# Side work of the first unit spread over later chunks, one table scatter per chunk, and matmuls of ones moved from the wait before the recurrent layer's output to the last down products

## The reference, cut to what matters

```
x = x + 0.5 * L0_ffn(layernorm(x))        # silu(x Wg) * (x Wu), hidden width 1024, then down to 256
x = x + L0_attn(layernorm(x))             # conv of 4 taps, two gates, linear recurrence over 512 steps, gelu gate
x = x + 0.5 * L0_ffn(layernorm(x))
x = x + 0.5 * L1_ffn(layernorm(x)) ...    # 8 experts; each adds 2048 deltas to a 256x256 matrix

# L0_attn: the decay is exp(-8 * sigmoid(gate) * softplus(a_param)), softplus on 256 numbers
# L1_ffn : deltas = softmax(expert_atom_weights) @ atoms     (8 x 2048)
#          weighted = deltas * sigmoid(importance)
#          added at (mask_idx // 256, mask_idx % 256); equal indices add up
```

## Time and profile before

| | us |
|---|---|
| three runs, median | 1249.54 |
| three runs, lowest and highest | 1244.13, 1250.32 |
| the profiled execution, its own time | 1241.68 |
| its span, first to last instruction | 1239.9 |
| TensorE busy | 1113.2 (90% of the span) |
| VectorE busy | 824.3 (66%) |
| GpSimd busy | 543.5 (44%) |
| mean granted TensorE clock | 0.973 |

### The profile page before, as it was taken

One profiled execution on the slowest core, in us unless ns is written; L12 is line 12 of the kernel. 1 busy time (PEld: TensorE's weight loads), 2 busy tenths in 40 slices (PEclk: granted clock), 3 DMA queues, 4 the chain that ended last, 5 costly groups with the idle time before them and its releaser, 6 DMA issues.

```text
span 1239.9 us, 22110 instructions
## 1 busy us (share of the span) xinstructions
PE 1113.2 (90%) x6837; PEld 939.2 (76%) x6837; DVE 824.3 (66%) x2280; ACT 603.3 (49%) x1420; POOL 543.5 (44%) x662
## 2 busy tenths in 40 slices
PE   3798779789989999998899989998899998999996
PEld 2677557677766778986676777896699997899995
DVE  3774456667888875567877876566766565665666
ACT  2234435351111334557766766555455554555552
POOL 4466445484045356126334434523354443544430
PEclk9899889899989999999999999999999999999999
DMA  6222413023003103433102144343001010010101
GB/s 212 90 66 59 156 39 132 26 79 115 1 1 139 47 18 120 132 97 81 39 13 46 42 158 153 120 145 115 27 28 49 25 51 26 26 51 25 51 1 34
DMA packets 48181, 87.83 MB, mean 71 GB/s; under 512 B 9504, under 2 KB 28320, under 8 KB 47520
## 3 DMA queue, kind: packets, MB, share of 16 engines
q1 hardware_dynamic: 41536, 72.98, 18.5%
q0 software_dynamic: 3968, 8.85, 2.4%
q10 hardware_dynamic: 2592, 4.92, 1.1%
HBM read 61.23 MB, written 19.20 MB: 65 GB/s over the span
## 4 chain that ended last, share of the span: by engine, by line
PE 60%; DVE 21%; ACT 8%; issue 5%; POOL 3%; DMA 2%; SPq 1%; ACTq 0%; DVEq 0%; POOLq 0%
PE ps L290 18%; PE ps L291 16%; PE ps L292 16%; DVE a_ptl L1925 4%; PE ps L1901 3%; DVE a_p L1860 2%; ACT a_pth L1917 2%; ACT a_p L1868 2%; DVE x L1614 1%; PE ps L460 1%; PE ps L940 1%; DMA att_bo<-in_att_bo 1%; DVE xl L454 1%; DVE x L1121 1%; DVE stats L336 1%
## 5 line engine op out<-in xcount | busy, mean ns | idle before, releaser
L1886 POOL TENSOR_SCALAR a_p<-a_p,small 128x128 f32<-128x128 f32 (+3 forms) x256 | 132.2, 534 | 218.2 <-DVE small L1877 218.1
L1868 ACT ACTIVATE a_p<-a_p,small 128x128 f32<-128x128 f32 (+3 forms) x256 | 141.6, 554 | 76.4 <-DVE small L1860 75.8
L290 PE MATMUL ps<-xh,wh 128*128 128x512 f32 x304 | 128.8, 424 | 31.5 <-DVE xl L454 17.9
L1925 DVE TENSOR_TENSOR a_ptl<-ps,a_pth 128x384 fp32r<-128x384 f32 (+1 forms) x192 | 106.6, 596 | 60.9 <-ACT a_pth L1917 60.4
L291 PE MATMUL ps<-xl,wh 128*128 128x512 f32 x304 | 124.8, 411 | 0.0
L292 PE MATMUL ps<-xh,wl 128*128 128x512 f32 x304 | 124.7, 410 | 0.0
L1917 ACT ACTIVATE a_pth<-ps 128x384 fp32r<-128x384 f32 (+1 forms) x192 | 90.4, 523 | 58.5 <-PE ps L1901 58.3
L1860 DVE CUSTOM_DVE_ANT_0 a_p<-ps,maskrow 128x128 f32<-128x128 f32 (+3 forms) x256 | 111.7, 483 | 4.0 <-PE ps L292 2.1
L402 POOL TENSOR_TENSOR rstd<-veps,nhalf 128x4 f32<-128x4 f32 x24 | 25.9, 1078 | 169.8 <-DVE veps L346 169.8
L290 PEld LDWEIGHTS ps<-xh,wh 128*128 128x128 f32 x304 | 60.3, 198 | 47.5 <-DVE xl L454 19.6
L1901 PE MATMUL ps<-ident,a_p 128*128 128x128 f32 x640 | 83.6, 277 | 5.4 <-DVE a_ptl L1925 2.2
(11 more groups left out here) (365 smaller groups left out, 3359.8 us busy)
## 6 DMA issues: line engine op xcount, KB each, us to landing
raw<-in_w SPq DMA_DIRECT2D x32, 384.0 KB, 3.1
raw<-in_qk SPq DMA_DIRECT2D x16, 512.0 KB, 3.5
raw<-moe_x SPq DMA_DIRECT2D x60, 128.0 KB, 2.4
moe_y<-m_y SPq DMA_DIRECT2D x60, 128.0 KB
m_raw<-in_ex SPq DMA_DIRECT2D x8, 608.0 KB, 7.8
m_a<-in_ex SPq DMA_DIRECT2D x8, 608.0 KB, 5.9
raw<-in_v SPq DMA_DIRECT2D x16, 256.0 KB, 2.6
moe_x<-drh SPq DMA_DIRECT2D x8, 480.0 KB, 5.6
```

Source lines behind the costliest of these rows:

```text
L290: pe.matmul(o, l[0], r[0], start=start, stop=False, skip_group_check=True)
L1868: s.activation(p[:, par, P_AT[i]:P_AT[i + 1]], p[:, par, P_AT[i]:P_AT[i + 1]], ACT.Exp, bias=h_nmx[:, par, i:i + 1], scale=scale, accum_ou ...
L1886: g.tensor_scalar(pp, pp, h_inv[:, par, i:i + 1], 1.0, ALU.mult, ALU.mult).then_inc(sem("at_norm"), 1)
L1925: ins = v.tensor_tensor(dst, ps[:, bank, 0:cols], f32(hi), ALU.subtract)
```

## The change

Eight edits, all in what units 0 to 5 carry:

- The softplus of the recurrent layer's parameter (`dve_softplus_start`, an exponential and a logarithm on ACT, `dve_softplus_rest`) moves from the start of the program and chunks 0, 1 and 3 to chunks 3, 4, 5, 6 and 7 of unit 0.
- In unit 0 the sigmoid of the importance goes from chunk 0 to chunk 2, the scatter's target indices (`d_dest`, `d_desti`) from chunk 0 to chunk 7, `trib` from chunk 0 to chunk 3.
- The first comparison is made in chunk 2 instead of chunk 1, and chunk 3 makes three.
- The constants of later layers (`dve_consts`) go from chunk 1 of unit 0 to chunk 5 of unit 5.
- The scatters: before, two per chunk of unit 1 and four behind them. After, one per chunk of unit 1, four behind them, and one per chunk of unit 4.
- The table's read is issued after chunk 7 of unit 4 instead of after chunk 2.
- `pe_rg_wait` goes. Twelve matmuls of ones stand between `down(6)` and `down(7)`, and twelve behind the transposes of the next unit, in units 1 and 4.
- In units 1 and 4 ACT makes the second half of the convolution's high part ahead of gelu instead of behind it.

These twelve are new there, and twelve more stand one `down` earlier. The diff:

```diff
@@ -698,11 +698,12 @@
                 gate_up(6)
                 down(5)
                 gate_up(7)
-                pe_rg_wait(pe, r)
                 pe_rg_out(pe, r)
                 down(6)
+                pe_warm(pe, 12, 2)
                 down(7)
                 pe_T(pe, 4 if u == 1 else 5)
+                pe_warm(pe, 12, 2)
             else:
                 down(0)
                 for j in range(2, CH0):
@@ -739,11 +740,9 @@
                 act_rg_x(s, r)
                 chunk(2)
                 act_rg_conv_hi(s, r, 0)
-                if u == 4:
-                    act_table(s)
                 chunk(3)
+                act_rg_conv_hi(s, r, 1)
                 act_rg_gelu(s, r)
-                act_rg_conv_hi(s, r, 1)
                 chunk(4)
                 act_rg_sigmoids(s, r, 0)
                 chunk(5)
@@ -753,6 +752,8 @@
                 act_rg_gated_hi(s, r)
                 chunk(6)
                 chunk(7)
+                if u == 4:
+                    act_table(s)
                 act_norm(s, 4 if u == 1 else 5)
                 act_T(s, 4 if u == 1 else 5)
             else:
@@ -1415,14 +1416,6 @@
                 mm3c(pe, ps[:, c, :], [rc(k * 512 + (DC + c) * P, P) for k in range(DC)], [xT(b, k) for k in range(DC)])\
                     .then_inc(sem("rg_xy"), 1)
 
-        def pe_rg_wait(pe, r):
-
-            b = r - 2
-            pe.wait_ge(sem("rg_sigm"), 4 * (b + 1))
-            for name, n in (("rg_th", 4), ("rg_sqrt", 8), ("rg_scan", 8), ("rg_g", 6)):
-                pe.wait_ge(sem(name), DC * (b + 1))
-                pe_warm(pe, n, 0)
-
         def pe_rg_out(pe, r):
             b = r - 2
             pe.wait_ge(sem("rg_glo"), DC * (b + 1))
@@ -2377,7 +2370,7 @@
         d_sg, d_wt, d_r1, d_r2, d_cmb = [d_work[:, k, :] for k in range(5)]
 
         QUARTERS = ((5, 0), (5, 1), (5, 3), (5, 4))
-        EQ_MASK = {1: [0, 1], 2: [2], 3: [3], 4: [4, 5, 6, 7], 5: [8, 9, 10, 11], 6: [12, 13, 14, 15]}
+        EQ_MASK = {2: [0], 3: [1, 2, 3], 4: [4, 5, 6, 7], 5: [8, 9, 10, 11], 6: [12, 13, 14, 15]}
         EQ_SUM = {4: [0, 1, 2, 3], 5: [4, 5, 6, 7], 6: [8, 9, 10, 11], 7: [12, 13, 14, 15]}
 
         def sp_delta_first(sp):
@@ -2433,7 +2426,10 @@
             if u == 0 and j == 0:
                 act_rg_weights(s, 2)
                 act_rg_weights(s, 3)
-            if u == 0 and j == 1:
+            if u == 0 and j == 4:
+                s.wait_ge(sem("sp_abs"), 1)
+                s.activation(sp_y, sp_abs, ACT.Exp, scale=-1.0).then_inc(sem("sp_y"), 1)
+            if u == 0 and j == 6:
                 s.wait_ge(sem("sp_u"), 1)
                 s.activation(sp_ln, sp_u, ACT.Ln).then_inc(sem("sp_ln"), 1)
             if (u, j) in QUARTERS:
@@ -2531,33 +2527,20 @@
                 v.wait_ge(sem("d_step"), d_steps[0])
 
             if u == 0 and j == 0:
-                v.wait_ge(sem("d_in"), 16 * 3)
-                v.wait_ge(sem("sp_y"), 1)
-                v.tensor_scalar(sp_u, sp_y, 1.0, None, ALU.add).then_inc(sem("sp_u"), 1)
-                then(v.tensor_copy(trib[:, :], d_trif[:, :]))
-                then(v.tensor_copy(d_row[:, :], d_rowi[:, :]))
-                then(v.tensor_copy(d_colf, d_col[:, 0, :]))
-
-                then(v.tensor_scalar(d_col[:, 1, :], d_col[:, 0, :], D - 1, 8, ALU.bitwise_and, ALU.logical_shift_left))
-                then(v.tensor_scalar(d_col[:, 2, :], d_col[:, 0, :], 8, None, ALU.logical_shift_right))
-            if u == 0 and j == 1:
-                dve_consts(v)
-            if u == 0 and j == 0:
                 v.wait_ge(sem("d_exp"), 1)
                 then(v.reciprocal(d_ri, d_sum))
                 settled()
-                then(v.tensor_tensor(d_col[:, 3, :], d_col[:, 1, :], d_col[:, 2, :], ALU.bitwise_or))
                 v.tensor_scalar(d_sm, d_sm, d_ri, None, ALU.mult).then_inc(sem("d_sm"), 1)
+                v.wait_ge(sem("d_in"), 16 * 3)
+                then(v.tensor_copy(d_row[:, :], d_rowi[:, :]))
+                then(v.tensor_copy(d_colf, d_col[:, 0, :]))
+            if u == 0 and j == 2:
+                v.wait_ge(sem("d_smt"), 1)
+                v.tensor_copy(d_smT, ps[0:NA, 1, 0:E]).then_inc(sem("d_smtc"), 1)
                 v.wait_ge(sem("d_exp"), 2)
                 then(v.tensor_scalar(d_sg, d_sg, 1.0, None, ALU.add))
                 settled()
                 then(v.reciprocal(d_sg, d_sg))
-                then(v.tensor_copy(d_dest, d_col[:, 3, :]))
-                settled()
-                v.tensor_copy(d_desti[:, :], d_dest).then_inc(sem("d_dest"), 1)
-            if u == 0 and j == 2:
-                v.wait_ge(sem("d_smt"), 1)
-                v.tensor_copy(d_smT, ps[0:NA, 1, 0:E]).then_inc(sem("d_smtc"), 1)
             if u == 0 and j == 3:
                 v.wait_ge(sem("d_delta"), 1)
                 settled()
@@ -2574,7 +2557,23 @@
                 then(v.tensor_tensor(r2, r1, d_wb[:, :, 8:16], ALU.subtract))
                 settled()
                 v.tensor_copy(d_wb[:, :, 16:24], r2).then_inc(sem("d_wb"), 1)
+                dve_softplus_start(v)
+                then(v.tensor_copy(trib[:, :], d_trif[:, :]))
+            if u == 0 and j == 5:
+                v.wait_ge(sem("sp_y"), 1)
+                v.tensor_scalar(sp_u, sp_y, 1.0, None, ALU.add).then_inc(sem("sp_u"), 1)
+            if u == 0 and j == 7:
                 dve_softplus_rest(v)
+                then(v.tensor_scalar(d_col[:, 1, :], d_col[:, 0, :], D - 1, 8, ALU.bitwise_and, ALU.logical_shift_left))
+                then(v.tensor_scalar(d_col[:, 2, :], d_col[:, 0, :], 8, None, ALU.logical_shift_right))
+                settled()
+                then(v.tensor_tensor(d_col[:, 3, :], d_col[:, 1, :], d_col[:, 2, :], ALU.bitwise_or))
+                settled()
+                then(v.tensor_copy(d_dest, d_col[:, 3, :]))
+                settled()
+                v.tensor_copy(d_desti[:, :], d_dest).then_inc(sem("d_dest"), 1)
+            if u == 5 and j == 5:
+                dve_consts(v)
             if u == 0 and j in EQ_MASK:
                 settled()
                 dve_equal(v, EQ_MASK[j])
@@ -2645,9 +2644,6 @@
             s.wait_ge(sem("d_max"), 1)
             s.activation(d_sm, d_ew, ACT.Exp, bias=d_max, accum_out=d_sum).then_inc(sem("d_exp"), 1)
             s.activation(d_sg, d_imp[:, :], ACT.Exp, scale=-1.0).then_inc(sem("d_exp"), 1)
-            s.wait_ge(sem("sp_abs"), 1)
-            s.activation(sp_y, sp_abs, ACT.Exp, scale=-1.0).then_inc(sem("sp_y"), 1)
-
         sp_abs, sp_y, sp_u, sp_v, sp_ln, sp_z, sp_m, sp_t = [small[:, 380 + 2 * k:382 + 2 * k] for k in range(8)]
 
         def pool_start(g):
@@ -2660,7 +2656,6 @@
         def dve_start(v):
             dve_ln(v, 0)
             dve_delta_max(v)
-            dve_softplus_start(v)
             dve_T(v, 0)
 
         def dve_consts(v):
@@ -2783,15 +2778,15 @@
             for i in range(1, CH0 // 2):
                 for p in range(2):
                     pool_chunks(g, 1, i, p)
-                    k = 4 * i + 2 * p - 4
-                    pool_scatter(g, [k, k + 1])
-            pool_scatter(g, range(12, NK))
+                    pool_scatter(g, [2 * i + p - 2])
+            pool_scatter(g, range(6, 10))
             pool_ln(g, 4)
             pre(4)
             pool_ln(g, 3)
             for i in range(1, CH0 // 2):
                 for p in range(2):
                     pool_chunks(g, 4, i, p)
+                    pool_scatter(g, [8 + 2 * i + p])
             pool_ln(g, 5)
             pre(5)
             pool_ln(g, 6)
```

## The result

The changed kernel took 1213.72 us (median of four runs, 1211.78 to 1219.51) beside 1247.45 for the kernel before, a ratio of 0.9738 with a 95% interval of 0.9692 to 0.9784. Run again it took 1216.99 (six runs), ratio 0.9778 (0.9744 to 0.9811). The forecast was 1211 in a range of 1203 to 1224. The profiled execution took 1215.54 with a span of 1213.3, against 1241.68 and 1239.9: 26.1 gained by time and 26.6 by span, where the sum of the terms was 34.3.

The account below looks back on a forecast made before the run. TensorE, busy 90% of the span, was taken as the bound, with gains only from its pauses, half clock and unread work. Terms 16.5 - 1.0 + 17.6 - 0.3 + 2.0 - 0.5 = 34.3 gave 1207.4, some 4 more 1211 us; range 1203 to 1224.

Parts of the forecast that it names:

- Start: Start of unit 0: constants leave the path, recurrent weights' landing comes next, first down product at 24.0 instead of 30.39 us.
- Chunk 0 to the first sums: Unit 0: atoms product at 32.4 us, first sums of comparisons at 40.5 instead of 59.05, a gain of 18.5.
- without the pause it should run at the high clock: Atoms product in unit 0's chunk 0: takes 3.7 us instead of 6.61 once TensorE no longer pauses ahead of it.
- ScalarE's waits for TensorE's gate product in each chunk cover it: Unit 0's chunks 4 and 6: exponential's and logarithm's table loads, about 2.8 each, cost nothing; without cover 5.6 us.
- Chunk 7: End of unit 0: softplus and target indices, 3.4 to 4.7 us less 2.08 idle, delay unit 1, taken as 2.0.
- Unit 1: Recurrent layer's first product to unit 4: single scatters per chunk make it unit 4's twin, 17.6 us gained.
- Ones: Units 1 and 4: recurrent output starts cold, -2.0; last down +1.2, next unit's first product +2.7; +2.0 us taken for both units.
- Unit 5's constants and the table's read: Constants between unit 5's products taken as -0.5 us; the table's later read in unit 4 taken as -0.3.
- The offset: Whole kernel: the new median expected some 4 us above the 1207.4 summed for an execution like the profiled one.
- The scatters hold unit 1's end: Rival, chance 0.13: four scatters behind chunk 7 delay unit 4's layer norm, up to 12 us late, about 1218.
- The loads do set the start: Rival, chance 0.10: crowded load queues put the first down at 26.8 or later, 3 to 6 us lost, 1216.
- The clock did come back: Rival, chance 0.10: clock stays low from recurrent output through the ones, nothing regained at next unit; 11 us together, 1222.

Follow-up runs that it names:

- `start_back`: Changed kernel with softplus' start and its exponential back ahead of unit 0, behind the last constant: 1224.67 us, ratio 0.9836.
- `after_again`: The changed kernel itself run once more, with nothing altered: 1216.99 us, ratio 0.9778.
- `ones_back`: Changed kernel with the 26 waiting ones back ahead of the recurrent output and the 24 new ones per unit removed: 1219.13 us, ratio 0.9807.
- `exp_early`: Changed kernel with softplus' exponential in chunk 3 on ScalarE and its start on VectorE in chunk 1: 1216.66 us, ratio 0.9790.
- `ones_none`: Changed kernel with no matmuls of ones at all in units 1 and 4: 1219.13 us, ratio 0.9794.
- `tail_exp`: Changed kernel with index work at chunk 0's front, softplus' rest in unit 1 and the exponential in chunk 3: 1211.18 us, ratio 0.9750.
- `scatter_alone`: Kernel before with only one scatter per chunk and the table's read moved behind chunk 7 of unit 4: 1225.79 us, ratio 0.9855.
- `tail_moved`: Changed kernel with VectorE's index work moved from chunk 7 to chunk 0's front and softplus' rest into unit 1: 1213.08 us, ratio 0.9750.
- `ones_both`: Changed kernel with the 26 waiting ones back ahead of the recurrent output and the 24 new ones per unit kept: 1212.47 us, ratio 0.9739.

## Why the prediction was right, and which terms were not

**Start.** Right: the constants left the path, the recurrent weights' landing took their place (ScalarE waits 3.72 us for it at 17.90), and the first down product came at 23.14 (24.0 predicted). `start_back` confirms it.

**Chunk 0 to the first sums.** The atoms product came at 33.30 and took 3.73 (32.4 and 3.7). The sums came at 42.84, not at 40.5: 0.9 from there, and 1.5 because the clock fell behind the atoms product. The step "without the pause it should run at the high clock" held for the product itself in this profile, not for what follows it, and not in every profile: 4.29 us in `after_again`, 5.26 at a clock of 0.68 in `ones_back`. With the clock at 1.00 throughout, as in `exp_early`, `ones_none` and `tail_exp`, it is 8.0 us from the product to the sums, which is what I had worked out (8.1); in the other profiles of the unspread product it was 9.5 to 11.1. The 59.05 that the gain of 18.5 was counted from was itself one execution; `scatter_alone`, with the same code up to there, had 54.92.

**Pitch of the sums.** The step "ScalarE's waits for TensorE's gate product in each chunk cover it" failed for the exponential: one normalization stands in the same gap. It cost 2.9 in the profiled execution and nothing in `after_again`, by where VectorE's comparisons fell beside GpSimd.

**Chunk 7.** "I take 2.0" was too small: 2.7 in the first profile and 3.5 in `after_again`, with unit 1's first products at a clock of 0.57. The cover of 2.08 us was as assumed; the work was not, 4.85 us instead of 3.4 to 4.7 (5.37 in `after_again`), since single small instructions take 0.5 to 1.25 us there, others each time. VectorE in order of time in the changed kernel, GpSimd beside it, then the longest of the tail in `after_again`, and then the first instruction in `tail_moved`, where GpSimd was idle:

```profile
69.02 1.12 DVE L2570 TENSOR_TENSOR d_col<-d_col 128x16 int32<-128x16 int32 x1
...
68.83 1.28 POOL L525 TENSOR_TENSOR wl<-raw,wh 128x512 fp32r<-128x512 f32 x1
```

```profile
68.39 1.25 DVE L2704 TENSOR_SCALAR rgp<-small 128x2 f32<-128x2 f32 x1
```

```profile
16.25 0.17 DVE L2540 TENSOR_TENSOR d_col<-d_col 128x16 int32<-128x16 int32 x1
```

The long one of the five index instructions is this time the bitwise one, not the last cast; in `after_again` these two took 0.17 and 0.18, the other cast 0.58, and the longest of the tail was a softplus row. So it is not the operation. It is what GpSimd is doing: all eleven rows over 0.25 us in the two tails start behind the start of a GpSimd instruction and end 0.00 to 0.03 us behind its end (69.02 + 1.12 beside 68.83 + 1.28; 68.39 + 1.25 beside 68.36 + 1.26). The Trainium skill ("Trainium Architecture — The Big Picture", What this means for kernel authors) has VectorE and GpSimd share a port as an exclusive lock; 1.12 beside GpSimd's 1.28 and 0.17 without it agree with that. So does the delay of 2.7, against the 2.6 that the prediction had by this rule and the 2.0 that it took.

These three make the mis-sized term: unit 0's gain was put at 16.5 and was 10.6. The missing 5.9 is 2.3 at the sums, 2.9 in the pitch and 0.7 in the tail; in `after_again` it is 4.8, nothing and 1.5. `tail_exp`, which removes the second and third and happened to keep the clock, begins unit 1 at 64.97, where I had 66.1 with 2.0 of tail in it.

**Unit 1.** Right: 17.4 (17.6 predicted), shown alone by `scatter_alone`. Its low clock at the start cost 0.7 (1.0).

**Ones.** Right in sum, 1.7 to 3.5 by `ones_back` and about 1.8 by the first profile (unit 1 nothing beside `scatter_alone`, unit 4's first products +2.4, unit 4's end -1.8, unit 5's first silu +1.2), against 2.0. A cold recurrent output was paid and the next unit's start given back, as written. The +1.2 at the last down appears against the old ones and not against none, as `ones_none` shows. The 5.58 in the sum ran to VectorE's product; TensorE's own first twelve matmuls took 5.28 before and 2.90 to 4.12 in the changed kernel.

**Unit 5's constants and the table's read**: nothing, where -0.8 was predicted. The constants do hold VectorE's product of chunk 6 (3.86 us behind the one before instead of 2.18), but from unit 5's first matmul to the first product with the table it took 42.07 us instead of 43.67, 0.4 better than the first silu's 1.2 alone. **Behind that product** the prediction had nothing; the profile is 29.6 ahead there and 26.6 at its end, and no run shows why. **The offset** of 4 between this profile and a median was wrong: the profiled execution lay 1.8 above the median. That took back part of the 8 us by which the sum was too high, so by luck the 1211 is nearer than its terms deserve.

**Rivals.** The scatters hold unit 1's end for 0.9, far from 12. The loads do set the start, but at the better end of the bounds. The clock did come back for unit 4's first products in both profiles of the changed kernel, and for unit 5's in one of two (0.71 in 207.50 to 211.00 of the first).

## What to carry to other kernels

When a wait is removed, the next limit is often the small work that it hid: price side work against the slack that will be left when its engine comes earlier, not the slack in the old trace. Mind, too, what GpSimd does in that place: a small VectorE instruction lasted here until the GpSimd instruction beside it had ended. A chain of waiting transfers belongs one link at a time into loops with room for each. Matmuls that nobody reads paid here in two places, in the wait ahead of the recurrent output, in groups that each wait for a step of the chain, and behind the transposes of the next unit; measure each place by itself.

## What the hardware showed that I had not expected

The granted clock fell while TensorE was busy without a break: 1.00 in 33.30 to 37.00, during 32 matmuls of 8 columns, then 0.85 and 0.64 up to 42.80 with 4.00 of 4.00 us busy. The same order of matmuls kept 1.00 in three other profiles (`exp_early`, `ones_none`, `tail_exp`), so it does not always happen; spread over a longer stretch it was worse (0.53). The stretch behind the product in `exp_early`:

```profile
36.70:41.00 4.30, 4.30 (x26) 3.58 (x25) 4.09 (x10) 3.12 (x4) 2.38 (x4) 1.00 0.36 126
```

Whether the narrow matmuls are the cause stays open, since no run left them out. The rule in the Trainium skill ("TensorE: Matmul & The Clock Gate", HAM oscillation — how this bites in real kernels), that pauses make the clock drop, agrees with 0.50 behind the 6.37 us pause; here the rows show no pause ahead of the fall.

The second is how VectorE and GpSimd hold each other up. The first of chunk 5's four comparisons on VectorE began ahead of a GpSimd split or at the very end of one and took 0.74 or 0.75 us. Each of the nine others in the changed kernel, its second profile and `ones_both` began while a split was under way and ended 0.54 to 0.56 us behind that split's end, whatever was left of it, and so took 0.89 to 1.75. That fits a comparison that stands still until the split is over.
